# Two transformer layers with experts: the down projection from half-precision parts, and the queries of the second attention in another order

## The chip, the cores and the metric

## The reference, cut to what matters

x is 64 x 64 x 128 (4096 tokens of width 128), ctx the same. Four blocks, each added to x times a gate:

```python
x = x + tanh(g_xattn[0]) * pooled_attention(layernorm(x), ctx)
x = x + tanh(g_ffn[0]) * experts_relu(layernorm(x))      # top 2 of 8
x = x + tanh(g_xattn[1]) * cross_attention(layernorm(x), ctx, mask)  # 16 heads of 8
x = x + tanh(g_ffn[1]) * experts_gelu(layernorm(x))
```

An expert is `act(x @ W1 + b1) @ W2 + b2` with W1 128 x 512 and W2 512 x 128. In the first experts block each token goes to its two best of eight experts with their biases; in the second one the 8192 sorted pairs of token and expert are cut into eight equal parts, one for each expert's weights, without biases.

## The kernel before, in words

Tokens lie 128 to a slot in 32 slots (X), eight chunks of 512 tokens (c) or four pairs of chunks (p). The first attention and the first routing run until about 200 us. Routing scatters a row for each token and choice (its value as two f16 parts, its number and its weight) to a list in memory sorted by expert (xs).

**Experts.** `experts(l)` exists once for every engine (PE line 912, ACT 1183, DVE 1607, POOL 521, SP 640). It takes tiles of 256 rows: 40 in layer 0, 32 in layer 1, in rounds of eight; the first and the last round are written out, those between are a hardware loop, in which the semaphore values that are waited for depend on the loop's register. SP loads a tile's rows; PE transposes them (`gather`, line 929); DVE copies them to SBUF (`parts`, line 1614); PE multiplies with w1 in 12 f16 matmuls of 256 columns (`up`: w1 high times both halves of x, w1 low times the high half, four chunks of FF); ACT applies relu or gelu (lines 1195, 1198) and writes `hid` in f32; PE multiplies with w2 (`down`, lines 942 to 951) in eight f32 matmuls of 128 columns, which the trace records as two each; DVE adds the bias (layer 0, line 1297), multiplies with the weight (line 1632) and POOL scatters the result to ys (line 528), after a 1x1 operation (line 526) that tells DVE of its turn. All matmuls have line 758, the helper `mm`. Which expert a tile has is read from a table in SBUF into a register: on PE twice per tile (`expert`, line 954), in layer 0 on ACT (1193) and DVE (1626) as well. Weights are then addressed by `ds(e * FF + c * D, D)`. The order on PE is written out by hand (`round_`, line 956):

```python
gather(i, q + 1)
up(i, q, expert(i * XS_LEAD + q))
down(i, q - 1, expert(i * XS_LEAD + q - 1))
```

and on DVE (line 1635): `parts(i, q + 1)`, then `result(i, q - 1)`.

**Between the experts.** After layer 0 DVE fills half of `kmask` with zeros (line 1668), turns the mask and fills v9 (1671 to 1679); ACT fills both halves of `qmask` (1211); SP loads ys (660); POOL adds the two rows of a token (551); DVE adds them to x (`combine`), normalises pair by pair (`norm`: lines 1302 to 1323); PE transposes (`query_transposed`, 991) and projects (`query_projected`), ACT and DVE take the high and the low f16 part (1226, 1603), SP stores them and loads them back in the layout of the scores, for `q3` and, blanked by head, for `qmask`.

**The attention loop** runs over g from -8 to 41 on PE, ACT and DVE, one slot of 128 tokens per step. `scores(g + 6)` feeds a maximum over keys (line 1712) six steps ahead; every four maxima are turned, stored and loaded back (max_rows) as an additional row of the next product; `scores_by_key(g)` gives the exponential (1236). In the order of before all four pairs of queries are projected ahead of or in the first step (`query(p)`, line 1004), and the first `scores_by_key` waits for all low parts. Routing of layer 1 and the splitting of its w1 run inside this loop; its scatters end in a wait of all engines, from about 600 to 640 us, which ends when rewritten rows have been stored and loaded. In that wait the first tiles of layer 1 already run from rows gathered by POOL (`head_gathered`).

## Time and profile before

| | |
|---|---|
| runs | 770.82, 771.95, 767.83 us; median 770.82 |
| profiled execution | 765.61 us, its span 763.8 us, mean granted clock 0.795 |
| busy, share of the span | PE 68%, PEld 56%, DVE 55%, ACT 31%, POOL 44% |
| experts of layer 0, 205 to 348 us | PE busy 138.66 of 143 us, clock 0.98 |
| queries, 358 to 427 us | PE busy 37.8 of 69 us, DVE 46.7 |
| experts of layer 1 after the wait, 641.3 to 735 us | PE busy 93.16 of 93.7 us, clock 0.98 |
| chain that ended last | PE 50%, DVE 24%, POOL 8%, issue 8%, DMA 6% |

### The profile page before, as it was taken

How to read it: one execution, taken by the hardware profiler on the slowest of the kernel's cores; microseconds unless marked ns; L12 is line 12 of the kernel's file. 1: busy time of each engine (PE TensorE's matmuls, PEld its weight loads, DVE VectorE, ACT ScalarE, POOL GpSimd, SP SyncE). 2: the span in 40 equal slices, each digit the busy share in tenths (PEclk: the TensorE clock that was granted, in tenths of full speed). 3: DMA queues.
4: the chain of work that ended last, by engine and by line, in shares of the span. 5: the costliest groups of instructions: out<-in, count | busy, mean ns of one | idle time of the engine just before them, and what ended most of it. 6: DMA issues, size and time to landing. Idle time of an engine off the chain costs nothing.

```text
span 763.8 us, 17097 instructions
## 1 busy us (share of the span) xinstructions
PE 518.3 (68%) x5273; PEld 428.3 (56%) x5274; DVE 416.7 (55%) x1454; ACT 235.4 (31%) x411; POOL 339.5 (44%) x424
## 2 busy tenths in 40 slices
PE   1587958423199999992387687777862076999950
PEld 1255745301199899991254466666651065989950
DVE  4785686987123333334895377878568611222215
ACT  0221011222044444443621365454631021232310
POOL 6212106777345656665500000071647676666650
PEclk9978876755599999997565599696765578999995
DMA  7911101124222222342763265353214123232219
GB/s 210 264 32 42 28 1 44 51 95 129 69 72 79 76 79 73 80 136 76 236 187 124 55 162 151 96 150 71 67 45 147 45 54 101 80 79 80 68 52 317
DMA packets 73194, 76.51 MB, mean 100 GB/s; under 512 B 12984, under 2 KB 61368, under 8 KB 73064
## 3 DMA queue, kind: packets, MB, share of 16 engines
q1 hardware_dynamic: 58504, 50.98, 24.4%
q0 software_dynamic: 10224, 22.40, 9.5%
q10 hardware_dynamic: 4400, 2.26, 1.0%
q8 instruction: 40, 0.66, 0.4%
q14 instruction: 26, 0.21, 0.1%
HBM read 46.15 MB, written 29.34 MB: 99 GB/s over the span
## 4 chain that ended last, share of the span: by engine, by line
PE 50%; DVE 24%; POOL 8%; issue 8%; DMA 6%; ACT 2%; SPq 1%; POOLq 0%; ACTq 0%; DVEq 0%
PE PS L758 46%; POOL xs L517 5%; DVE XN L1323 3%; DVE stats L1302 3%; DMA work<-ys 3%; DVE X L1297 2%; PE PS L929 2%; DVE work L1712 2%; DVE work L1297 1%; POOL work L565 1%; DVE rtmp L1297 1%; DVE mv L1305 1%; DVE nwt L1297 1%; PE PS L1074 1%; DMA work<-max_rows 1%
## 5 line engine op out<-in xcount | busy, mean ns | idle before, releaser
L517 POOL DMA_INDIRECT xs<-pack,adr_i x80 | 78.7, 983 | 197.8 <-ACT pack L1147 142.0
L528 POOL DMA_INDIRECT ys<-work x144 | 140.7, 977 | 34.5 <-issue 34.5
L758 PE MATMUL PS<-w,work 128*128 x1152 | 143.8, 279 | 3.0 <-issue 1.7
L758 PEld LDWEIGHTS PS<-w,work 128*128 128x128 f32 x1152 | 134.9, 193 | 9.0 <-issue 6.8
L758 PE MATMUL PS<-work,w1h 128*128 128x256 f16 x576 | 103.1, 281 | 1.1 <-issue 1.1
L1195 ACT ACTIVATE work<-PS,b 128x256 f32<-128x256 f32 x160 | 62.7, 474 | 95.5 <-PE PS L758 69.2
L1297 DVE TENSOR_TENSOR work<-PS,work 128x256 f32<-128x256 f32 (+3 forms) x82 | 33.0, 405 | 94.7 <-issue 55.6
L758 PE MATMUL PS<-work 97*64 97x256 f16 (+5 forms) x608 | 74.0, 318 | 15.4 <-DVE work L1429 7.6
L758 PE MATMUL PS<-work,w1l 128*128 128x256 f16 x288 | 80.9, 281 | 0.0
L758 PEld LDWEIGHTS PS<-work 97*64 97x64 f16 (+2 forms) x608 | 56.0, 163 | 25.9 <-DVE work L1429 10.9
L1632 DVE TENSOR_SCALAR work<-PS,work 128x128 f32<-128x128 f32 x64 | 19.5, 346 | 79.0 <-PE PS L758 79.0
L929 PE MATMUL PS<-ident,work 128*128 128x128 f16 x288 | 29.5, 228 | 47.2 <-DMA work<-xs,headadr_i 24.6
L758 PEld LDWEIGHTS PS<-work,w1h 128*128 x576 | 54.7, 101 | 8.4 <-issue 2.1
L1712 DVE TENSOR_REDUCE work<-PS 128x16 f32<-128x1024 f32 x32 | 39.1, 1222 | 33.8 <-PE PS L758 33.8
L1198 ACT ACTIVATE work<-PS 128x1024 f32<-128x1024 f32 x32 | 32.8, 1024 | 80.2 <-PE PS L758 80.1
L758 PE MATMUL PS<-work,W 128*128 128x512 f32 x60 | 48.4, 933 | 8.1 <-DVE work L1297 3.4
L517 POOL DMA_INDIRECT xs<-work,adr_i x48 | 47.1, 981 | 14.8 <-issue 13.6
L1614 DVE COPY work<-PS 128x512 f16<-128x512 f16 x72 | 30.1, 418 | 39.7 <-PE PS L929 39.5
L929 PEld LDWEIGHTS PS<-ident,work 128*128 128x128 f16 x288 | 22.8, 102 | 50.7 <-issue 39.6
L526 POOL TENSOR_TENSOR turn<-lane 1x1 f32<-1x1 f32 x72 | 17.3, 240 | 72.6 <-DVE work L1632 72.4
L1236 ACT ACTIVATE XN<-PS,mask_bias 128x1024 f32<-128x1024 f32 x32 | 35.6, 1113 | 19.1 <-PE PS L758 18.9
L758 PE MATMUL PS<-ident,work 128*64 128x36 f32 x512 | 25.9, 255 | 22.7 <-DVE work L1297 22.7
(259 smaller groups left out, 809.8 us busy)
## 6 DMA issues: line engine op xcount, KB each, us to landing
work<-xs SPq DMA_DIRECT2D x132, 65.0 KB
work<-ys SPq DMA_DIRECT2D x12, 512.0 KB, 5.9
k_parts<-work SPq DMA_DIRECT2D x24, 128.0 KB
w<-k_parts SPq DMA_DIRECT2D x8, 384.0 KB
work<-k_parts SPq DMA_DIRECT2D x32, 96.0 KB
work<-q_parts SPq DMA_DIRECT2D x8, 384.0 KB
work<-q_parts SPq DMA_DIRECT2D x32, 96.0 KB
ys<-work POOLq DMA_INDIRECT x144, 2.3
```

The source lines that it names most:

```text
L517: g.indirect_dma_start(xs[l], bass.IndirectOffsetOnAxis(adr_i[:, k, T:T + 1], 0), pack_of(l, c)[:, s, k, :].bitcast(U32), None)\
L528: g.indirect_dma_start(ys[l], bass.IndirectOffsetOnAxis(xin[:, q, u, :].bitcast(U32)[:, D:D + 1], 0), yrow[:, q, u, :], None).then_inc(ff[ ...
L758: return t.matmul(o, lhsT, rhs, start=start, stop=stop, skip_group_check=True)
L929: ins = t.transpose(o[:, h, u, :], xin[:, q, u, h * D:(h + 1) * D], ident16[:])
L1195: ins = a.activation(hid[:, v, c, :], PF[:, b * 512 + c * TILE:b * 512 + (c + 1) * TILE], ACT.Relu, bias=b1[:, ds(e * FC + c, 1)], scale=1 ...
L1198: ins = a.activation(hid[:, v, :, :].rearrange("p c n -> p (c n)"), banks(b, 1024), ACT.Gelu, scale=1 / WSCALE)
L1236: a.activation(pexp[:, T % 2, :], banks(2, 1024), ACT.Exp, bias=mask_bias[:, T:T + 1]).then_inc(p_done, 1)
L1297: return v_.tensor_tensor(o, x, y, op)
L1302: ins = v_.bn_stats(stats[:, T, :], X[:, T, 0:D])
L1323: ins = v_.tensor_scalar(XN[:, slot + s, :], X[:, T, 0:D], mv[:, T, 0:1], rstd[:, T:T + 1], ALU.subtract, ALU.mult)
L1614: v_.tensor_copy(xgT[:, v, :, :].rearrange("p h n -> p (h n)"), PS[:, v, 0:TILE].bitcast(F16))\
L1712: v_.tensor_reduce(rmaxq[:, c % 2, s, :], banks(0, 1024).rearrange("p (h k) -> p h k", h=H), AX, ALU.max).then_inc(s_max, 1)
```

## The change

**Down from parts.** `hid` is written in f32 as before; ACT copies it to f16 (`hid_hi`), DVE forms `hid_lo` = hid - hid_hi in two halves of 128 rows (`low`), each with a semaphore step. w2 is scaled by 256 and split in place of XN into high and low f16 parts before each layer's experts, by ACT (`w2_hi`) and DVE (`split_w2`); gates and b2 carry the scale. `down` makes, for each half u, eight matmuls with `hid_hi` (high and low part of w2 for each of four chunks), waits for `lo`, and makes four with `hid_lo`. DVE's order per tile becomes `result(q - 2)`, `parts(q + 1)`, `low(q - 1)`.

**Blanking.** b2 is loaded after the first attention to another place; the mask's preparation, both halves of `kmask`, and w2's split come before layer 0's experts on DVE. One half of `qmask` is filled by DVE, with v9, once all rows of layer 0 are scattered; the other by ACT.

**Queries.** Pair 0 is projected first; pair 1 is transposed in the attention loop's first step and projected in its step g = -3, pair 2 at g = -1 and 0, pair 3 at g = 1. DVE's maxima 0 to 5 stand between combine, statistics, roots and rows of the pairs. The queries use only the first 16 slots of XN, in turn; banks differ, small tiles of the maxima move to `big1`. SP stores, loads keys, queries, blocks and w1 in the new order.

The diff, cut to its core:

```diff
-b2b = at(104, [E * D])
+b2b = at(44, [E * D])
...
+hid_hi = at(48, [2, FC, TILE], F16)
+hid_lo = at(68, [2, FC, TILE], F16)
+w2_parts = XN[:].rearrange("p t d -> p (t d)").bitcast(F16)
...
-BANK_Q, BANK_K, BANK_X3, BANK_LG = (2, 5), (4, 5), (3, 4), 6
+BANK_K, BANK_LG = (4, 5), 6
+BANK_X3, BANK_Q = (3, 4, 3, 4, 3, 4, 5, 7), (2, 5, 2, 5, 5, 7, 5, 7)
...
+    sp.wait_ge(x1_done, NC)
+    sp.dma_start(b2b, A["b2"].partition_broadcast(P)).then_inc(w_late, 16)
...
+    sp.wait_ge(mask_rows, 1)
+    sp.dma_start(mask_dram, mask16[:]).then_inc(mask_out, 16)
...
-    for c in range(2):
-        load_keys(c)
-    for c in range(NC):
+    def queries_stored(c):
...
-        if c == 1:
-            for k in range(2):
-                load_queries(k)
-            load_blocks(0)
-        elif c == 3:
-            load_blocks(1)
-    for c in range(NC):
...
+    sp.wait_ge(mask_out, 16)
+    load_keys(0)
+    y_load(0, 6)
+    y_load(0, 7)
+    load_keys(1)
+    queries_stored(0)
+    queries_stored(1)
...
+    load_queries(0)
+    load_queries(1)
+    load_blocks(0)
+    queries_stored(2)
+    load_keys(2)
+    load_queries(2)
+    queries_stored(3)
+    load_blocks(1)
+    queries_stored(4)
+    queries_stored(5)
+    w1_load(0)
+    for c in range(1, NC):
...
-        if c >= 1:
-            load_max(c)
+        load_max(c)
+        if c == 1:
+            w1_load(1)
...
-        w1_load(c)
+        if c == 1:
+            queries_stored(6)
+            queries_stored(7)
+        else:
+            w1_load(c)
...
-        if l == 1:
-            pe.wait_ge(w2_in, 16)
...
-            v, m = q % 2, (i + i0) * (XS_LEAD // 2) + q // 2
-            pe.wait_ge(f["hid"][v], m + 1)
+            v, m, tile = q % 2, (i + i0) * (XS_LEAD // 2) + q // 2, (i + i0) * XS_LEAD + q
+            if q == 0 and isinstance(i, int) and i == 0:
+                pe.wait_ge(w2_lo, (l + 1) * E)
+            pe.wait_ge(f["hi"][0], tile + 1)
...
+                o = PS[:, 6 + v, u * D:(u + 1) * D]
...
-                    ins = mm(PS[:, 6 + v, u * D:(u + 1) * D], hid[:, v, c, u * P:(u + 1) * P],
-                             w2[:, ds(e * FF + c * D, D)], start=c == 0, stop=c == FC - 1)
+                    for part in range(2):
+                        mm(o, hid_hi[:, v, c, u * P:(u + 1) * P],
+                           w2_parts[:, ds(e * 2 * FF + part * FF + c * D, D)], start=c + part == 0, stop=False)
+                pe.wait_ge(f["lo"][0], 2 * tile + u + 1)
+                for c in range(FC):
+                    ins = mm(o, hid_lo[:, v, c, u * P:(u + 1) * P],
+                             w2_parts[:, ds(e * 2 * FF + c * D, D)], start=False, stop=c == FC - 1)
...
+        if c >= 6:
+            pe.wait_ge(qk_lo, NC + c - 1)
+        if c == 7:
+            pe.wait_ge(nT_sb, 2)
...
-            ins = t.transpose(PS[:, BANK_X3[c % 2], s * P:(s + 1) * P], XN[:, c * CT_TILES + s, :], ident[:])
+            ins = t.transpose(PS[:, BANK_X3[c], s * P:(s + 1) * P], XN[:, slots(1, c).start + s, :], ident[:])
...
-        if c >= 2:
-            pe.wait_ge(qk_lo, NC + c - 1)
+        if 2 <= c < 5:
+            pe.wait_ge(qk_lo, NC + (0, 0, 1, 2, 4)[c])
+        if c == 5:
+            pe.wait_ge(v9_sb, 1)
...
-        mm(PS[:, BANK_Q[c % 2], :], wq1T, xnT1[:, c % 2, :]).then_inc(qk_ps, 1)
+        mm(PS[:, BANK_Q[c], :], wq1T, xnT1[:, c % 2, :]).then_inc(qk_ps, 1)
...
-    def query(p):
+    def queries_transposed(p):
...
+    def queries_projected(p):
...
-    for p in range(NP - 1):
-        query(p)
+    queries_transposed(0)
+    queries_projected(0)
...
-                pe.wait_ge(qk_lo, 2 * NC)
-                pe.wait_ge(zero, 1)
-                mm(WEIGHTED_PS, zrow[:, 0:P], zrow[:, 0:HG * SEQ])
+                pe.wait_ge(x3t_sb, 5)
+                pe.wait_ge(qk_lo, NC + 3)
...
+        if g == 0:
+            queries_projected(2)
...
-            query(NP - 1)
+            queries_transposed(1)
+        if g == -1:
+            queries_transposed(2)
+        if g == 1:
+            pe.wait_ge(zero, 1)
+            mm(WEIGHTED_PS, zrow[:, 0:P], zrow[:, 0:HG * SEQ])
+        if g == 2:
+            pe.wait_ge(qk_lo, 2 * NC)
...
+            if k == 1:
+                pe.wait_ge(qk_lo, NC + 6)
...
+        if g == 3 - LEAD:
+            queries_projected(1)
+        if g == 1:
+            queries_transposed(3)
+            queries_projected(3)
...
+        act.wait_ge(w_late, 16 * NL)
+        act.wait_ge(pack_lo, (l + 1) * NC)
+        if l == 1:
+            act.wait_ge(w2_in, 16)
+        for e in range(E):
+            a.activation(w2_parts[:, e * 2 * FF:e * 2 * FF + FF], w2[:, e * FF:(e + 1) * FF], ACT.Copy,
+                         scale=WSCALE).then_inc(w2_hi, 1)
...
-        act.wait_ge(w_late, 16 * NL)
...
-            v, m = q % 2, (i + i0) * (XS_LEAD // 2) + q // 2
+            v, m, tile = q % 2, (i + i0) * (XS_LEAD // 2) + q // 2, (i + i0) * XS_LEAD + q
...
-            wait(act, f["y"][v], m)
+            if not isinstance(i, int) or tile >= 2:
+                act.wait_ge(f["lo"][0], 2 * tile - 2)
...
+            act.wait_ge(f["hid"][v], m + 1)
+            wait(act, f["y"][v], m)
+            a.activation(hid_hi[:, v, :, :], hid[:, v, :, :], ACT.Copy).then_inc(f["hi"][0], 1)
...
-    for u in range(2):
-        blanked(qmask[:, u, :, :, :], q_blank)
-    for p in range(NP):
+    blanked(qmask[:, 0, :, :, :], q_blank)
...
+    def queries_transposed(p):
...
-            a.activation(xnT1[:, c % 2, :], PS[:, BANK_X3[c % 2], :], ACT.Copy).then_inc(x3t_sb, 1)
+            a.activation(xnT1[:, c % 2, :], PS[:, BANK_X3[c], :], ACT.Copy).then_inc(x3t_sb, 1)
...
+    def queries_high(p):
...
-            a.activation(q16[c][:, 0, :], PS[:, BANK_Q[c % 2], :], ACT.Copy, scale=QK_SCALE[0])\
+            a.activation(q16[c][:, 0, :], PS[:, BANK_Q[c], :], ACT.Copy, scale=QK_SCALE[0])\
...
+    queries_transposed(0)
+    queries_high(0)
+    queries_transposed(1)
...
+        if g == -1:
+            queries_transposed(2)
+        if g == 0:
+            queries_high(2)
...
+            if T == 0:
+                act.wait_ge(x_ff[0], 7)
...
+        if g == 3 - LEAD:
+            queries_high(1)
+        if g == 1:
+            queries_transposed(3)
+            queries_high(3)
...
+            v_.tensor_scalar(gt[:, 2:4], gt[:, 2:4], 1 / WSCALE, None, ALU.mult)
...
+        def low(i, q):
+            v, m = q % 2, (i + i0) * (XS_LEAD // 2) + q // 2
+            dve.wait_ge(f["hi"][0], (i + i0) * XS_LEAD + q + 1)
+            wait(dve, f["y"][v], m)
+            for u in range(2):
+                half = slice(u * P, (u + 1) * P)
+                tt(hid_lo[:, v, :, half], hid[:, v, :, half], hid_hi[:, v, :, half], ALU.subtract)                            .then_inc(f["lo"][0], 1)
...
+                if q >= 2:
+                    result(i, q - 2)
+                elif not first:
+                    result(i - 1, XS_LEAD + q - 2)
+                late = first and l == 1 and q == HEAD0 - 1
+                if late:
+                    low(i, q - 1)
...
-                    result(i, q - 1)
+                    if not late:
+                        low(i, q - 1)
...
-                    result(i - 1, XS_LEAD - 1)
+                    low(i - 1, XS_LEAD - 1)
...
+        result(rounds_ - 1, XS_LEAD - 2)
+        low(rounds_ - 1, XS_LEAD - 1)
...
+    def split_w2(l):
+        for e in range(E):
+            hi, lo = (w2_parts[:, (2 * e + part) * FF:(2 * e + part + 1) * FF] for part in range(2))
+            dve.wait_ge(w2_hi, l * E + e + 1)
+            v_.scalar_tensor_tensor(out=lo, in0=w2[:, e * FF:(e + 1) * FF], scalar=WSCALE, in1=hi,
+                                    op0=ALU.mult, op1=ALU.subtract).then_inc(w2_lo, 1)
...
-    v_.memset(kmask[:, 0, :, :, :], 0.0).then_inc(k_blank, 1)
-    experts(0)
-    dve.wait_ge(tails, 16 * E)
-    v_.memset(kmask[:, 1, :, :, :], 0.0).then_inc(k_blank, 1)
...
+    v_.tensor_scalar(b2b, b2b, WSCALE, None, ALU.mult)
+    split_w2(0)
+    v_.memset(kmask[:, 0, :, :, :], 0.0).then_inc(k_blank, 1)
+    dve.wait_ge(tails, 16 * E)
+    v_.memset(kmask[:, 1, :, :, :], 0.0).then_inc(k_blank, 1)
+    experts(0)
+    for q in range(XS_LEAD):
+        dve.wait_ge(ff["stored"][q], STORED * rounds[0])
...
-    for p in range(NP):
-        for c in (2 * p, 2 * p + 1):
-            combine(0, c)
+    v_.memset(qmask[:, 1, :, :, :], 0.0).then_inc(q_blank1, 1)
...
+    def maxima(T):
+        c, s = T // CT_TILES, T % CT_TILES
+        dve.wait_ge(s_ps, T + 1)
...
+        if s == CT_TILES - 1:
+            dve.wait_ge(s_max, T + 1)
...
+                dve.wait_ge(nT_ps, c)
+            link(v_.tensor_scalar(nmax.rearrange("p (r s j) -> p s r j", j=HG, r=HG),
...
+            tt(nmax16[:, 1, :], nmax, nmax16[:, 0, :], ALU.subtract).then_inc(n_ready, 1)
...
+    def query_rows(p):
+        if p >= 2:
+            dve.wait_ge(x3t_ps, 2 * p - 2)
+        norm_std(pair(p))
+        norm_rows(pair(p), slots(1, 2 * p).start, xn3)
...
+    for p in range(2):
+        combine(0, 2 * p)
+        combine(0, 2 * p + 1)
...
-        norm(pair(p), pair(p).start, xn3)
-        if p >= 1:
-            parts_of_projection(2 * p - 2)
-            parts_of_projection(2 * p - 1)
-    for g in range(G0, G1):
-        k = g + LEAD - 1
-        if k in (0, 1):
-            parts_of_projection(NC - 2 + k)
-        if k == 2:
+        norm_stats(pair(p))
+        if p == 1:
+            parts_of_projection(0)
+            parts_of_projection(1)
+        norm_root(pair(p))
+        if p == 1:
+            maxima(0)
+        query_rows(p)
+    maxima(1)
+    combine(0, 4)
+    maxima(2)
+    combine(0, 5)
+    maxima(3)
+    dve.wait_ge(x_ff[0], 6)
+    norm_stats(pair(2))
+    maxima(4)
+    parts_of_projection(2)
+    parts_of_projection(3)
+    norm_root(pair(2))
+    maxima(5)
+    query_rows(2)
+    combine(0, 6)
+    combine(0, 7)
+    dve.wait_ge(x_ff[0], 8)
+    norm_stats(pair(3))
+    parts_of_projection(4)
+    parts_of_projection(5)
+    norm_root(pair(3))
+    for g in range(G1):
+        if g == 2:
...
-            c, s = T // CT_TILES, T % CT_TILES
-            dve.wait_ge(s_ps, T + 1)
...
-            if s == CT_TILES - 1:
-                dve.wait_ge(s_max, T + 1)
-                if c >= 1:
-                    dve.wait_ge(nT_ps, c)
-                link(v_.tensor_scalar(nmax.rearrange("p (r s j) -> p s r j", j=HG, r=HG),
...
-                link(v_.tensor_copy(nmax16[:, 0, :], nmax))
-                tt(nmax16[:, 1, :], nmax, nmax16[:, 0, :], ALU.subtract).then_inc(n_ready, 1)
+            maxima(T)
+        if g == 0:
+            query_rows(3)
+        if g == 1:
+            parts_of_projection(6)
+            parts_of_projection(7)
```

## Rows read from the trace of the kernel before

**Rows 1.** The page's first part: busy us, share of the span, instructions.

```profile
PE 518.3 (68%) x5273; PEld 428.3 (56%) x5274; DVE 416.7 (55%) x1454; ACT 235.4 (31%) x411; POOL 339.5 (44%) x424
```

**Rows 2.** Windows: us, busy by engine, PE's granted clock, DMA share, GB/s.

```profile
265.10:292.70 27.60, 27.20 (x256) 25.45 (x256) 9.90 (x33) 12.53 (x32) 16.93 (x24) 1.00 0.28 77
641.30:735.00 93.70, 93.16 (x859) 87.20 (x860) 24.43 (x79) 27.64 (x27) 57.50 (x81) 0.98 0.27 74
...
378.00:403.00 25.00, 21.51 (x94) 14.93 (x94) 23.77 (x113) 7.28 (x13) 0.00 (x0) 0.70 0.56 172
403.00:427.00 24.00, 14.32 (x70) 9.30 (x69) 9.83 (x13) 3.22 (x6) 0.00 (x0) 0.50 0.45 134
```

**Rows 3.** Timeline of PE, layer 0: start, length, engine, line, operation, tiles, shapes, count.

```profile
226.50 0.27 PE L758 MATMUL PS<-work,w1l 128*128 128x256 f16 x1
226.61 1.95 PE L758 MATMUL PS<-w,work 128*128 x16
228.40 0.39 PE L929 MATMUL PS<-ident,work 128*128 128x128 f16 x4
...
229.93 1.95 PE L758 MATMUL PS<-w,work 128*128 x16
```

**Rows 4.** Source views, 640.2 to 643.6: count, duration ns, first and last start.

```profile
L758 PEldq FUSED_REGOPS  x4: 46/46/46, 641.2 to 641.9; - x4
...
L758 PEldq ALU_OP  x4: 32/32/32, 641.3 to 642.0; - x4
...
L954 PEldq TENSOR_LOAD <-eidx_i x2: 306/350/395, 640.3 to 642.3; - x2
...
L758 PEldq FUSED_REGOPS  x4: 46/46/46, 643.0 to 643.4; - x4
```

**Rows 5.** Source view of line 954 in a dense stretch of layer 1.

```profile
L954 PEldq TENSOR_LOAD <-eidx_i x3: 297/298/301, 688.6 to 691.9; - x3
```

**Rows 6.** Timelines of ACT, DVE and PE, layers 0 and 1.

```profile
227.49 1.56 ACT L1195 ACTIVATE work<-PS,b 128x256 f32<-128x256 f32 x4 [1.75 <-PE PS L758]
...
229.34 0.42 DVE L1297 TENSOR_TENSOR work<-PS,work 128x256 f32<-128x256 f32 x1 [2.05 <-PE PS L758]
...
230.20 0.42 DVE L1614 COPY work<-PS 128x512 f16<-128x512 f16 x1
...
686.27 1.95 PE L758 MATMUL PS<-w,work 128*128 x16
...
688.46 0.61 DVE L1632 TENSOR_SCALAR work<-PS,work 128x128 f32<-128x128 f32 x2 [2.38 <-PE PS L758]
```

**Rows 7.** Groups by line: busy us, mean ns of one, idle before.

```profile
L1297 DVE TENSOR_TENSOR pack<-XN,pack 128x512 f16<-128x512 f32 x10 | 6.8, 684 | 0.0
...
L1143 ACT ACTIVATE pack<-XN 128x512 f16<-128x512 f32 x10 | 6.1, 626 | 6.7 <-DVE XN L1323 6.7
```

**Rows 8.** Timeline of DVE at the start of layer 0.

```profile
205.24 0.42 DVE L1614 COPY work<-PS 128x512 f16<-128x512 f16 x1 [12.64 <-PE PS L929]
```

**Rows 9.** Timelines after layer 0, and the chain there (start, us, what).

```profile
350.21 4.29 POOL L526 TENSOR_TENSOR turn<-lane 1x1 f32<-1x1 f32 x1 [0.48 <-DVE work L1632]
...
350.92 3.47 DVE L1668 MEMSET work<- 128x4096 uint32 x1 [0.80 <-issue]
...
358.70 5.11 DMA work<-ys
```

**Rows 10.** Timeline of DVE at 373, and the chain from 400 to 440.

```profile
373.80 3.08 DVE L1323 TENSOR_SCALAR XN<-X,mv,rstd 128x128 f32<-128x128 f32 x8
...
415.41 1.24 DVE work L1712
...
421.19 5.73 DMA work<-max_rows
...
427.06 1.09 PE PS L758 x8
...
431.44 1.24 DVE work L1712
```

58 lines of the change are left out of this document (32 added, 26 removed).

## The prediction

> **What bounds the kernel now.** The page first: no engine is busy for more than 68% of the span [rows 1], so each stage has to be read by itself. The windows by stage [rows 2] show experts stages in which PE is busy 99% of the time at a granted clock of 1.00 and 0.98, which is the full one of its two levels (2.4 GHz); in the query stage between them DVE is busy 23.8 of 25 us and then 9.8 of 24, with PE at 0.70 and 0.50. So experts follow PE; the queries follow DVE, and after it a chain of waits.
>
> One tile in the timeline [rows 3]: up's last matmul, the 16 records of down, four transposes, the next down. Down starts at 226.61, the transposes at 228.40: 1.79 us for eight f32 matmuls, 0.112 a record. The next down starts at 229.93: **a tile is 3.32 us**. In the loop's rounds eight tiles (256 PE records) take 27.6 us, 3.45 each [rows 2].
>
> Behind the array stands its sequencer, whose rows (PEldq) are not counted as busy. After 640.3 the array had been idle, and nothing but its own work held the sequencer [rows 4]: it loads the expert's number at 640.3; up's eight address operations run from 641.2 to 642.0, 0.12 apart whether they take 46 or 32 ns; the second load is at 642.3; down's four run from 643.0 to 643.4, again 0.12 apart. With down's remainder (0.1) and the start of the next gather that is about 3.2 us a tile. In the dense stage its rhythm is that of the tile: three loads from 688.6 to 691.9, two per tile [rows 5]. **So array (3.32) and sequencer (3.2) are nearly equal**, and in loop rounds, where the thresholds of waits are register values too, the same matmuls already take 0.13 longer.
>
> **The change, part by part.**
>
> Down on the array: 24 f16 matmuls of 128 columns instead of 8 of f32. The nearest row has their shape, the four transposes: 0.39 for four of which the last one's 0.22 counts once, so 0.056 each [rows 3]. 24 x 0.056 = 1.34 against 1.79: the array would need 2.87 us a tile, 0.45 less. The Trainium skill ("TensorE: Matmul & The Clock Gate", Back-to-back issue gap) gives about 81 ns for a matmul of N=128 in a stream of load and matmul pairs; by that down would take 1.94, a tile of the array 3.5, and the sum below would be some 8 us higher, an estimate by that page. The row speaks against it, though for four in a row only.
>
> Down on the sequencer: weights are addressed by expert, part and chunk, eight addresses instead of four. Up shows one operation for two matmuls with the same address (8 for 12), down one for both u (4 for 8), so I count 4 more a tile: 4 x 0.12 = 0.5. A tile then needs 3.2 + 0.5 + 0.05 for two more waits = 3.75. Computed afresh at every use it would be 20 more, 2.4 us; hidden by something I don't see, 0. In loop rounds the thresholds tile + 1 and 2 tile + u + 1 are new in every tile, three more at 0.12: 3.35 + 0.5 + 0.36 = 4.2.
>
> Down's new inputs. ACT copies hid to f16 behind relu: 1024 elements, 1.05, from 0.63 for 512 [rows 7] with the fixed part taken once. In layer 0 relu starts at 227.49, 0.72 after up ends (226.50 + 0.27), since the expert's number is loaded there too, and takes 1.57: 3.4 in all, under the tile. In layer 1 1.02 and 1.05. DVE forms the low part in halves of 512 elements, 0.68 each [rows 7], 1.3 for both. Its order becomes result(q-2), copy(q+1), low(q-1); result waits for a down that waited for a low: **a ring DVE, PE, DVE**. In layer 0 [rows 6] down's end (226.61 + 1.95) to the add at 229.34 is 0.78, the add to the end of the copy is 1.28, low 1.3, less overlap: 3.3 from down's end to low's. In layer 1 down's end (686.27 + 1.95) to 688.46 is 0.24, then 0.9 and 1.3: 2.4.
>
> PE's side: from low's end the sequencer issues the last matmuls, gather, load, up's addresses, load, its 3.75 less the 1.0 of down's eight addresses = 2.75 until down can begin. Then eight matmuls paced by addresses (1.0), 16 at 0.056 (0.9), 0.2 to the end: 2.1. Between two turns of the ring lie two tiles: layer 0 (2.1 + 3.3 + 2.75)/2 = 4.1; layer 1 (2.1 + 2.4 + 2.75)/2 = 3.6, under the sequencer's 3.75. In loop rounds layer 0 has 0.4 of thresholds more per turn: 4.3.
>
> Experts in sum. Layer 0: 16 tiles x (4.1 - 3.32) + 24 x (4.3 - 3.45) = 12.5 + 20.4 = 33. Layer 1: six tiles run before 640 in the shadow of the rewritten rows; 10 x (3.75 - 3.32) + 16 x (4.2 - 3.45) = 4.3 + 12 = 16. In each layer's last tile copy, low and down stand in series, +1 each. **Together +51.** Bounds: with free addresses layer 0 still goes by DVE's part of the ring (3.3 + 0.4 = 3.7: +15) and layer 1 by the array (26 x 0.4 = -10), +5; with 20 operations +160.
>
> Moved ahead of layer 0 on DVE: mask work (1.3), b2's scaling (0.7), eight low parts of w2 (5.5, at 0.69), one more memset (3.5), 11 us in all. DVE has been idle for 12.6 us when the first tile's copy starts at 205.24 [rows 8], and PE and DVE wait there for the scatters: hidden, 1.6 to spare, and beyond that it delays the first tile. ACT's eight copies (0.63) run beside. Before layer 1 the same splitting lies in the wait that ends at 640.3: nothing. On SP b2's DMA moves behind the residual and ahead of the tails, the mask's store ahead of the wait for the scatters, y's chunks 6 and 7 between key loads, where they are used last: nothing, between 0 and +2.
>
> Memset after layer 0: a 1x1 operation on POOL took 4.29 [rows 9], over the whole of DVE's 3.47 memset, and the last scatter waited behind it. That memset is now earlier: -4.1. In return v9's memset (2.0) and one of qmask (3.5) run while y loads (5.1) and hold DVE and POOL's sums some: +1.8. ACT blanks for 7 us instead of 14, not waited for.
>
> Queries in the order of need. Before [rows 10], pair 0's rows end at 376.9, the other pairs follow, the maxima wait for them and the fourth ends at 416.65, and the first scores by key start at 427.06, 5.7 of the 10.4 us being DMA; the seventh maximum is at 431.4. After, by the same durations less 2.3: pair 0's rows to 374.6, low parts of chunks 0 and 1 to 380.4, pair 1's root to 383, first maximum at 387 after store and load, pair 1's rows and the maxima to 398.7, so the chain would allow 409. But DVE has 17 us for pairs 2 and 3 meanwhile, and comes to the seventh maximum at 417, -14.4; pair 3's rows and low parts (3.4) and PE's last pair (2) are then still to do. -9, the memset's in it; rounded to -10, between 0 and -22 (DVE's 14 idle us, the memset, part of the DMA chain).
>
> **Sum:** 765.6 (the profiled execution: span 763.8 and 1.8 around it) + 51 - 10 = 807. The runs' median of before is 770.8, 5 above that execution; I leave the 807.
>
> **Rivals.**
> *Addresses are hidden.* Then the experts cost +5 and the queries give up to 16: 755. For it: an operation is 46 ns long. Against: 0.12 apart even with an empty array. The place is PE's sequencer between low and up, and it decides if one address costs under 0.03.
> *It cancels:* half hidden (+25), queries at their bound (-22): 769.
> *The clock falls.* PE would work 2.87 of 4.1 us; 99% busy goes with 1.00, 21.5 of 25 with 0.70 [rows 2]. Matmuls at half clock add 1.6 a tile where it happens; in a third of 66 tiles +35: 842.
> *Every use computes its address:* about 920.
>
> **Chances.** Forecast 0.62 (785 to 828, its own range); as forecast but only to 775 to 785, 0.08; clock 0.08; every use 0.04; cancels 0.06; hidden 0.12. The range leaves out the last, the clock and every use but for their nearest parts: 768 to 828. 0.5% is about what a measurement can tell from no change. Faster 0.12, same 0.06, slower 0.82.
>
> **What would show it.** Twelve to sixteen address operations a tile at the matmul's line; tiles of 4.1 and 3.75 us, longer in loop rounds; PE busy under 85% there; eight matmuls of down spaced 0.12, the rest 0.056; the 4.29 on POOL gone; the seventh maximum 14 us nearer to layer 0's end. Tiles of 3.0 in layer 1 would say that the sequencer never was a bound and the forecast is wrong.

## The result, and the profile after

| | before | after |
|---|---|---|
| runs | 767.83 to 772.11, median 771.38 us | 833.45 to 837.97, median 833.75 us |
| ratio | | 1.083, 95% interval 1.078 to 1.088 |
| profiled execution, its span | 765.61, 763.8 | 833.45, 831.7 |
| mean granted clock | 0.795 | 0.803 |

The change costs 8.3%. The forecast was 807, and 833.75 lies above the range. The page's first part, to be held against [rows 1]:

```profile
PE 545.0 (66%) x5849; PEld 414.8 (50%) x5850; DVE 514.2 (62%) x1617; ACT 312.7 (38%) x498; POOL 366.8 (44%) x424
```

PE was given less array work a tile, and is busy longer. DVE gained 98 us, ACT 77. The groups name the new work and its pauses:

```profile
L780 PE MATMUL PS<-XN,work 128*128 (+1 forms) x2752 | 173.3, 230 | 27.9 <-issue 21.5
L533 POOL DMA_INDIRECT ys<-work x144 | 164.8, 1145 | 34.3 <-issue 34.3
...
L1375 DVE TENSOR_TENSOR work<-work 128x512 f16<-128x512 f32 (+1 forms) x152 | 98.9, 690 | 5.9 <-ACT work L1262 5.6
...
L1262 ACT ACTIVATE work<-work 128x1024 f16<-128x1024 f32 x72 | 76.1, 1057 | 2.3
```

Most of PE's pauses before down's matmuls end with "issue": no other engine was late, its own sequencer was. **One tile**, in the source view of a loop round of layer 0 (294.0 to 298.3; count, duration ns, first and last start). L780 is the helper that issues every matmul, so its thirteen operations are down's eight, four of up's and the first of the next down:

```profile
L780 PEldq FUSED_REGOPS  x13: 46/46/60, 294.0 to 298.2; - x13
...
L780 PEldq ALU_OP  x4: 32/32/32, 296.5 to 297.2; - x4
...
L982 PEldq TENSOR_LOAD <-eidx_i x2: 302/303/304, 295.6 to 297.4; - x2
```

So sixteen address operations a tile, eight for up and eight for down, and two loads. Windows of loop rounds of both layers (columns as in [rows 2]), of the stretch between first and fourth maximum, and of the queries that follow:

```profile
265.10:298.22 33.12, 28.91 (x305) 22.41 (x303) 18.31 (x47) 19.97 (x38) 18.73 (x23) 1.00 0.24 65
711.60:776.10 64.50, 56.77 (x605) 44.66 (x603) 32.11 (x76) 31.21 (x30) 37.35 (x46) 1.00 0.23 62
425.00:437.00 12.00, 5.30 (x32) 3.16 (x32) 8.49 (x18) 1.20 (x2) 0.00 (x0) 0.50 0.04 15
437.00:478.00 41.00, 31.69 (x181) 22.69 (x183) 22.70 (x85) 10.67 (x18) 0.00 (x0) 0.58 0.36 99
```

The clock stays at its full level in the experts with PE busy 87 and 88%. In the queries it is at the lower level, 1.2 GHz, or little above it in the mean.

**Where the 68 us between the two profiled spans lie**, by the starts of single instructions in both traces: first load of the first tile's expert number 206.80 to 213.31 (+6.5); from there to the last load of layer 0 136.7 to 170.1 (+33.4); to the first exponential 84.6 to 72.4 (-12.3); to the fifth 14.2 to 29.5 (+15.3); to the last 122.0 to 126.3 (+4.3); layer 1's tiles, from the load at 640.3 to the last one, 92.6 to 112.5 (+19.9); the rest +0.8.

Of the +6.5 some 5 are not the change's: from 62 to 86 us, where both kernels do the same, the granted clock was 0.72 in the execution of before and 0.61 in that of after, and it was 0.61 as well in a kernel of the experiments whose code up to there is that of before and whose first load comes at 212.0. The other 1.7 are the change's. While DVE splits w2, POOL's scatters of the routing take 1.4 to 1.5 us instead of 0.97:

```profile
196.31 1.51 POOL L522 DMA_INDIRECT xs<-work,adr_i  x1 [0.30 <-issue]
198.12 1.50 POOL L522 DMA_INDIRECT xs<-work,adr_i  x1 [0.30 <-issue]
```

From the first to the last of these 64 scatters 83.5 to 83.8 us pass in all six kernels that split w2 there, 81.9 to 82.4 in twelve of the thirteen that do not. **Experts +53.3, queries +7.** The forecast had +51 and -10. Of the queries' +7 the last +4.3, from the fifth exponential to the last, is no more than executions with the same instructions in that stretch differ by: 119.4, 122.0 and 126.2 us in the kernel before and two kernels that differ from it in the experts alone.

**The query stage** in the chain of waits (start, us, what), where [rows 10] stood before:

```profile
398.94 3.69 POOL work L556
...
424.80 1.22 DVE big L1802
...
437.49 7.81 PE PS L780 x28
445.39 1.22 DVE big L1802
...
454.73 4.08 PE PS L780 x20
...
462.55 1.22 DVE big L1802
...
469.84 11.65 PE PS L780 x92
...
497.74 4.13 issue
```

The first maximum now follows 35.4 us behind POOL's last turn in layer 0 instead of 53.0. Of these 17.6 us 4.1 are the last turn itself, which took 4.29 [rows 9] and now takes 0.15. Then the chain runs through PE: 7.8 us between the fourth and fifth maxima, 4.1 ahead of the seventh, 11.7 ahead of the fourth exponential, of which 7.0 are the projections of pair 3, in front of what the third waits for. PE's timeline says what stands there, the projections of pairs 1 and 3, each chunk 2.05 for the queries and 1.71 for the router's logits at half clock:

```profile
437.30 2.05 PE L780 MATMUL PS<-work,W 128*128 128x512 f32 x2
439.14 1.71 PE L780 MATMUL PS<-wrc,work 128*128 128x8 f32 x8
...
469.68 2.07 PE L780 MATMUL PS<-work,W 128*128 128x512 f32 x2
471.54 1.72 PE L780 MATMUL PS<-wrc,work 128*128 128x8 f32 x8
```

### The profile page after: what moved, and what is told of

Its sections match the earlier page's. It is cut to its first block, busy times and chain, and to the rows that moved or that the text cites. A ratio compares the mean times of both kernels' runs of the same rounds, so it can differ in the third digit from the quotient of the medians.

```text
span 831.7 us, 19026 instructions
## 1 busy us (share of the span) xinstructions
PE 545.0 (66%) x5849; PEld 414.8 (50%) x5850; DVE 514.2 (62%) x1617; ACT 312.7 (38%) x498; POOL 366.8 (44%) x424
## 4 chain that ended last, share of the span: by engine, by line
PE 51%; DVE 21%; issue 11%; POOL 8%; DMA 6%; ACT 2%; SPq 1%; POOLq 0%; ACTq 0%; DVEq 0%
PE PS L780 46%; POOL xs L522 5%; DMA work<-ys 2%; DVE big L1802 2%; DVE XN L1410 2%; DVE stats L1379 2%; PE PS L949 2%; DVE X L1375 2%; DVE work L1375 1%; POOL work L570 1%; DVE rtmp L1375 1%; PE PS L1023 1%; DVE mv L1385 1%; DVE nwt L1375 1%; PE PS L1110 1%
## 5 line engine op out<-in xcount | busy, mean ns | idle before, releaser
L780 PE MATMUL PS<-XN,work 128*128 (+1 forms) x2752 | 173.3, 230 | 27.9 <-issue 21.5
L533 POOL DMA_INDIRECT ys<-work x144 | 164.8, 1145 | 34.3 <-issue 34.3
L780 PEld LDWEIGHTS PS<-XN,work 128*128 128x128 f16 (+1 forms) x2752 | 136.7, 102 | 73.4 <-issue 55.4
L780 PE MATMUL PS<-work,w1h 128*128 128x256 f16 x576 | 102.2, 280 | 10.1 <-issue 8.1
L1375 DVE TENSOR_TENSOR work<-work 128x512 f16<-128x512 f32 (+1 forms) x152 | 98.9, 690 | 5.9 <-ACT work L1262 5.6
L780 PE MATMUL PS<-work 97*64 97x256 f16 (+5 forms) x608 | 78.1, 327 | 24.5 <-DVE work L1517 7.5
L780 PE MATMUL PS<-work,w1l 128*128 128x256 f16 x288 | 80.2, 278 | 0.0
L1262 ACT ACTIVATE work<-work 128x1024 f16<-128x1024 f32 x72 | 76.1, 1057 | 2.3
L780 PEld LDWEIGHTS PS<-work 97*64 97x64 f16 (+2 forms) x608 | 58.5, 168 | 35.9 <-DVE work L1517 10.8
L780 PEld LDWEIGHTS PS<-work,w1h 128*128 x576 | 51.7, 100 | 25.7 <-issue 19.1
L1802 DVE TENSOR_REDUCE big<-PS 128x16 f32<-128x1024 f32 x32 | 39.1, 1222 | 34.7 <-PE PS L780 34.6
L522 POOL DMA_INDIRECT xs<-work,adr_i x48 | 48.7, 1014 | 15.3 <-issue 13.7
L780 PE MATMUL PS<-work,W 128*128 128x512 f32 x60 | 48.9, 941 | 8.1 <-DVE work L1375 3.4
L949 PEld LDWEIGHTS PS<-ident,work 128*128 128x128 f16 x288 | 20.0, 102 | 49.5 <-issue 42.7
```

Of the source, the lines that this page charges most:

```text
L522: g.indirect_dma_start(xs[l], bass.IndirectOffsetOnAxis(adr_i[:, k, T:T + 1], 0), pack_of(l, c)[:, s, k, :].bitcast(U32), None)\
L533: g.indirect_dma_start(ys[l], bass.IndirectOffsetOnAxis(xin[:, q, u, :].bitcast(U32)[:, D:D + 1], 0), yrow[:, q, u, :], None).then_inc(ff[ ...
L780: return t.matmul(o, lhsT, rhs, start=start, stop=stop, skip_group_check=True)
L949: ins = t.transpose(o[:, h, u, :], xin[:, q, u, h * D:(h + 1) * D], ident16[:])
L1262: a.activation(hid_hi[:, v, :, :], hid[:, v, :, :], ACT.Copy).then_inc(f["hi"][0], 1)
L1375: return v_.tensor_tensor(o, x, y, op)
```

## The experiments

Theories for the experts: (1) PE's sequencer, by addresses, loads and thresholds, and in layer 0 a ring with DVE; (2) the array or the number of matmuls; (3) DVE's low parts alone. For the queries: PE's projections in the loop, the clock, DVE's memsets beside POOL, SP's order.

### The new query stage alone

Down, its inputs and `result` are put back to f32 in the changed kernel (`w2_parts`, `split_w2`, `low` and ACT's copies gone); the rest stays.

> The query stage of the changed kernel with the experts' down as before (f32, four addresses a tile, no parts of w2 or hid). What is left of the difference to before is the query stage alone. If the pieces read from the two traces are right (experts +53, query stage +7), the time is 833.75 - 53 = 780 us, about 8 above before. If the prediction's sum is right for the stage (-10) and the experts cost more than they show, it is 761. Tiles at 3.3 us again in both layers.

775.44 us against 767.59 of before, ratio 1.0104 (1.0058 to 1.0149). So the stage costs some 8 us and the experts 1.0831 - 1.0104, or 56. The reading of the traces holds, and the forecast's -10 is where it failed.

### Down's weights at a fixed address

```
-   w2_parts[:, ds(e * 2 * FF + part * FF + c * D, D)]
+   w2_parts[:, part * FF + c * D:part * FF + c * D + D]
```

> The changed kernel with down's weights always taken from expert 0 at addresses that are constants (that expert's weights stand in for the chosen one's; both loads of the expert's number stay). Eight address operations a tile are gone, 24 matmuls stay. Theory 1, PE's sequencer sets the tile: it falls from 4.15 by 8 x 0.12 = 1.0 to 3.2 in layer 1, and in layer 0 to the ring of DVE and PE at 3.6 to 3.7: 833.75 - 22 - 25 = 787 us. Theory 2, the array or the number of matmuls sets it: unchanged, 834. Theory 3, the ring with DVE's low parts sets both layers: layer 0 unchanged, at most -10.

Every tile is then multiplied with expert 0's w2, so the output is no longer that of the reference; number and shape of the instructions stay. 802.51 us, 1.0471 (1.0389 to 1.0552), 28 under the changed kernel by the ratios; expected were 47. The rate of the tiles is read from POOL's one small operation a tile, in the source view of its line, first over the 24 loop tiles of layer 0, then over the 16 of layer 1. Before the change:

```profile
L526 POOL TENSOR_TENSOR turn<-lane x24: 182/183/184, 244.5 to 323.6; 1x1 f32<-1x1 f32 x24
...
L526 POOL TENSOR_TENSOR turn<-lane x16: 182/183/183, 661.1 to 712.5; 1x1 f32<-1x1 f32 x16
```

After the change:

```profile
L531 POOL TENSOR_TENSOR turn<-lane x24: 182/183/184, 259.1 to 357.5; 1x1 f32<-1x1 f32 x24
...
L531 POOL TENSOR_TENSOR turn<-lane x16: 182/183/184, 711.6 to 776.1; 1x1 f32<-1x1 f32 x16
```

With the fixed address:

```profile
L531 POOL TENSOR_TENSOR turn<-lane x24: 182/183/184, 253.4 to 346.1; 1x1 f32<-1x1 f32 x24
...
L531 POOL TENSOR_TENSOR turn<-lane x16: 182/183/641, 697.6 to 748.6; 1x1 f32<-1x1 f32 x16
```

Span over count less one: 3.44 and 3.43 before, 4.28 and 4.30 after, 4.03 and 3.40 here. Layer 1 gives back 0.90 a tile for eight addresses, 0.11 each, with all 24 matmuls still there: theory 1, against 2. Layer 0 gives back 0.25 only: there something else stands at 4.0.

### Rounds written out; one load a tile

```
-   with pe.Fori(1, n - 1) as i:
+   for i in range(1, n - 1):
```

and the same on SP, ACT, DVE and POOL.

> The changed kernel with the rounds of tiles written out instead of looped, on every engine: the thresholds of waits are constants, the addresses stay. Theory 1 (sequencer, thresholds at 0.12 each, about 3 a tile on PE): 24 tiles of layer 0 give 0.1 to 0.3, 16 of layer 1 0.4: 833.75 - 6 to - 14, so 820 to 828 us. If thresholds are free: 834.

821.31 us, 1.0677 (1.0582 to 1.0773), 12 under the changed kernel. Loop tiles are 4.11 and 3.85, by the same rows as above.

```
-   down(i, q - 1, expert(i * XS_LEAD + q - 1))
+   down(i, q - 1, numbers[q - 1])
```

> The changed kernel with the expert's number kept in its register from up to the down of the same tile, so that PE loads it once a tile instead of twice (seven of eight tiles). Theory 1 (sequencer: a load holds it 0.6 to 0.75 us): tiles from 4.15 to 3.5; in layer 0 the ring with a PE part of 2.0 instead of 2.75 gives 3.7: 833.75 - 16 - 17 = 800 us. Theory 2 (array) or 3 (DVE): at most -5.

814.36 us, 1.0606 (1.0506 to 1.0706), 17 under. Loop tiles 4.13 and 3.77; layer 1's last eight come at 3.20, from 3.74. So loops and loads are the sequencer's as well: in layer 1 0.45 a tile for the thresholds and whatever else a loop costs, 0.53 for seven eighths of a load. Layer 0 stays at 4.1 in both, which fits the prediction's ring.

### The ring in layer 0

Both edits together, and in layer 0 DVE's `low(i, q - 1)` ahead of `result(i, q - 2)`.

> The changed kernel with rounds written out, one load of the expert's number a tile, and in layer 0 DVE's low part of a tile ahead of the result of the tile before it. Theory 1 (sequencer in layer 1, DVE's ring in layer 0): layer 1's tiles go to 3.2 to 3.3 us, layer 0's from 4.1 to the ring by ACT (up 1.7, two ACT operations 3.4, down 2.2, over two tiles: 3.65) or a little above, 3.75: 833.75 - 20 - 18 = 795 us, 1.035 of before. Theory 2, layer 0 is held by ACT or POOL already: layer 0 stays at 3.9 to 4.1, 805 us, 1.045. Layer 1 at the array's 2.87 would say that only the sequencer held it, 3.2 that something else is near.

793.48 us, 1.0349 (1.0304 to 1.0394), as expected:

```profile
L531 POOL TENSOR_TENSOR turn<-lane x24: 182/183/185, 251.6 to 337.6; 1x1 f32<-1x1 f32 x24
...
L531 POOL TENSOR_TENSOR turn<-lane x16: 183/185/732, 687.1 to 736.9; 1x1 f32<-1x1 f32 x16
```

3.74 and 3.32. The result of the tile before, its load of the expert's number included, had stood between ACT's copy and the low part for which PE waits. Layer 0's tile falls by 0.37 from the 4.11 of written-out rounds alone, but most of that is not the new order's. The first and the last round are written out in the kernel with one load as well, so they have both edits without the order: turns there are 3.86 and 3.87 apart (the layer's last tile left out), with the order 3.81 and 3.76. So the order is worth 0.05 to 0.1 a tile, and the rest is what the two edits give together. That the ring of DVE and PE sets layer 0 is argued from its sum, not shown by this run. Layer 1 does not reach the array's estimated 2.87, and the window of its last tiles in the kernel with one load (columns as in [rows 2]) has a candidate for what is next:

```profile
763.00:785.00 22.00, 20.30 (x252) 17.86 (x249) 14.33 (x33) 12.48 (x12) 17.53 (x21) 1.00 0.17 52
```

POOL is busy 17.5 of 22 us, and with the pauses that end with "issue" between its operations (0.5 a tile) it has under 0.2 a tile left: two scatters of 1.15 each, a turn of 0.25. Before the change a scatter took 0.98. Two other readings remain. The sequencer's own 3.74 less 0.57 for the load is 3.17; but with the fixed address, which takes 0.9 from the sequencer, the last tiles are no faster, at 3.22. And whether PE or ACT would go on at 3.2 with shorter scatters was not tried.

### Was the sequencer the bound before?

```
+   expert(i * XS_LEAD + q)
    up(i, q, expert(i * XS_LEAD + q))
```

in the kernel before.

> The kernel before with one load more of the expert's number on PE in each tile, its value not used. Nothing else changes. This tests the premise of the prediction, that PE's sequencer (3.2 us a tile) stands just behind the array (3.32) before the change. Theory 1: a load holds the sequencer 0.6 to 0.75 us, so it becomes the bound at 3.8 to 3.95: 40 tiles of layer 0 and 26 of layer 1 take 0.4 to 0.5 more, +26 to +33 us, 1.034 to 1.043 of before. Theory 2, the sequencer had slack, the array stays the bound: +0 to +5, 1.000 to 1.006.

808.7 us, 1.0554 (1.0489 to 1.062), +42: above both expectations. Tiles:

```profile
L526 POOL TENSOR_TENSOR turn<-lane x24: 182/183/185, 252.9 to 347.3; 1x1 f32<-1x1 f32 x24
...
L526 POOL TENSOR_TENSOR turn<-lane x16: 182/183/183, 689.1 to 751.0; 1x1 f32<-1x1 f32 x16
```

4.10 and 4.13, so +0.66 and +0.70 for one load; where two loads follow each other they start 0.65 apart. Nothing was hidden: in loop rounds the sequencer was not just behind the array but the bound itself. In the written-out last rounds the tile grows by 0.5 to 0.6 (3.32 to 3.81, 3.19 to 3.77), so there it did have about 0.1 of slack, as the prediction said. The counterpart takes from it, in the kernel before, by rounds written out and one load a tile:

> The kernel before with rounds of tiles written out and one load of the expert's number a tile (seven of eight). The prediction's reading was that PE's sequencer (3.2 us a tile) stands just behind the array (3.32) and loses 0.13 a tile in loop rounds. If so: 24 tiles x 0.12 in layer 0 and 16 x 0.1 to 0.2 in layer 1 come off, -4 to -6: 0.993 to 0.995 of before. If the array alone sets the tile, or DVE and ACT in loop rounds: 1.000.

```profile
L526 POOL TENSOR_TENSOR turn<-lane x24: 182/184/185, 248.8 to 325.2; 1x1 f32<-1x1 f32 x24
...
L526 POOL TENSOR_TENSOR turn<-lane x16: 182/183/184, 663.3 to 713.1; 1x1 f32<-1x1 f32 x16
```

3.32 in both, the array's tile, 0.12 under before in the mean of the 40 loop tiles. Before, most of that lies where one round ends and the next begins: turns there are 4.27 to 4.41 apart, the others mostly 3.2 to 3.6. So it is mostly one pause of about 1 us a round, not 0.13 at every tile's thresholds. The time, 762.76 us against 770.14 with a ratio of 0.9975 (0.9923 to 1.0026), shows no gain that is clear of noise.

### The memsets moved ahead of layer 0, alone

```
+   v_.memset(kmask[:, 0, ...], 0.0).then_inc(k_blank, 1)
+   dve.wait_ge(tails, 16 * E)
+   v_.memset(kmask[:, 1, ...], 0.0).then_inc(k_blank, 1)
    experts(0)
```

with the mask work, b2's load and the mask's store moved as in the change.

> The kernel before, with one part of the change alone: the mask work and both memsets of kmask ahead of layer 0 on DVE (b2's load moved behind the residual and the mask's store ahead of the tails, as the change has them). The prediction's step: the moved work is hidden in the wait for the scatters, and the 4.29 us that POOL's last turn took are gone: -4, 767 of 771 (0.995 of before). Rival: the y load, not the memset, ends last, or the moved work delays the first tile: 1.000 or above.

760.95 us against 768.05, 0.9903 (0.9865 to 0.994). A gain, under 2%, and by its interval somewhat more than the 4 us of the expectation. In the chain of waits POOL's last turn, 4.29 in [rows 9], is an ordinary one:

```profile
354.84 0.18 POOL turn L526
355.02 0.16 issue
355.18 0.98 POOL ys L528
```

and the first maximum follows 49.1 us behind it instead of 53.0.

### DVE's memset beside POOL's sum

In the kernel of the new stage alone ACT zeroes both halves of qmask.

> The same kernel (new query stage, f32 down), with ACT zeroing both halves of qmask as before the change, so that DVE has only v9's memset left while y loads. Theory 1: DVE's memsets hold POOL's first sum of y at 3.69 us instead of 1.25: -1 to -3.5 us, 1.006 to 1.009 of before. Theory 2: the y load ends last there: unchanged, 1.010. If ACT's second zeroing (5 to 7 us) reaches its first copy of the queries: slower.

773.63 us, 1.0093 (1.0061 to 1.0125): not to be told from 1.0104. The row it was about did change. POOL's second sum of y after the change, and DVE's memset over it:

```profile
398.94 3.68 POOL L556 TENSOR_TENSOR work<-work 128x512 f32<-128x512 f32 x1 [0.21 <-DMA work<-ys]
...
397.50 3.47 DVE L1797 MEMSET work<- 128x4096 uint32 x1 [0.92 <-issue]
```

and here:

```profile
359.13 1.64 POOL L556 TENSOR_TENSOR work<-work 128x512 f32<-128x512 f32 x1 [0.21 <-DMA work<-ys]
```

2.0 us less at that place, too little for the times.

### The clock

28 and then 6, 6, 6 matmuls of 256 columns ahead of the first four scores, in the kernel of the new stage alone.

> The kernel of the run with f32 down (new query stage alone, 1.0104 of before), with extra matmuls on PE where it waits: 28 of 256 columns ahead of the first scores, 6 ahead of each of the next three, into a PSUM bank that is overwritten later. Nothing is left out. Theory 1: the projections of pair 1 run at half clock because PE has idled before; with the clock up they take 3.5 instead of 7.0 us, and as they delay the fifth scores the stage gives back 3.5 (up to 8 if the clock stays up): 1.000 to 1.006 of before. Theory 2, DVE's order sets the stage: unchanged, 1.010. If the extra matmuls are themselves in the way: 1.015 or more.

778.1 us, 1.0146 (1.0102 to 1.019): no gain, and rather a loss. The windows show that PE's clock did rise for the projections of pair 1, and was down again for those of pairs 2 and 3:

```profile
390.00:400.00 10.00, 7.36 (x52) 4.26 (x51) 7.04 (x16) 0.78 (x2) 0.00 (x0) 0.84 0.01 3
400.00:410.00 10.00, 6.58 (x34) 4.88 (x32) 5.97 (x24) 1.96 (x4) 0.00 (x0) 0.67 0.28 66
410.00:420.00 10.00, 9.11 (x33) 5.98 (x33) 5.40 (x19) 3.42 (x5) 0.00 (x0) 0.50 0.74 226
```

Pair 1 took 4.9 us (397.64 to 402.56) instead of 7.0; pair 2, 3.9 us in the kernel after the change, took 7.0. What one place gained the next lost. What the stage would take at full clock throughout, no run shows.

### The logits out of the chain, and SP's order

```
    mm(PS[:, BANK_Q[c], :], wq1T, xnT1[:, c % 2, :]).then_inc(qk_ps, 1)
-   for s in range(CT_TILES): ... wrc ...
+   (for pairs 1 to 3: behind scores(g + LEAD) of g = -1, 0, 2)
```

> The kernel of the new query stage alone (f32 down, 1.0104 of before), with PE's small matmuls for the router's logits of pairs 1 to 3 (8 columns each, 1.7 us a chunk at half clock) taken from between the projections to behind the next scores, and DVE's use of them one turn later. Nothing is left out. Theory 1, PE's projections in the loop lie in series between maxima and exponentials: each of three places in the chain gives up to 3.4 us: -7 to -10, 0.998 to 1.002 of before. Theory 2, DVE's order or the loads of q and max_rows end last there: at most -2, 1.008 to 1.010.

771.92 us, 1.0103 (0.9991 to 1.0215), the time of the kernel without the edit. DVE's use of the logits moves with them, to one step later. From POOL's last turn to the third exponential 81.8 us pass, against 88.3 in the changed kernel (88.6 with the extra matmuls, 89.2 with ACT's zeroing); to the ninth 110.1 against 113.6; to the last 222.4 against 222.2. The gain of 6 to 7 us is gone by the end of the stage. The wait that took a part of it, in the chain:

```profile
427.68 9.84 PE PS L780 x92
...
453.71 4.97 issue
```

"Issue" here is a DMA that the chain doesn't name. In the kernel after the change the same place is a wait of PE's sequencer of 4.5 us at `scores_by_key`, for the rows of maxima, and SP's timeline says why they are late: the six stores of chunks 6 and 7 and four block loads go first.

```profile
487.11 2.97 SPq L601 DMA_DIRECT2D q_parts<-w1l  x6
490.19 3.46 SPq L682 DMA_DIRECT2D work<-q_parts  x4
493.75 1.21 SPq L448 DMA_DIRECT2D max_rows<-big  x2
497.68 0.29 SPq L451 DMA_DIRECT2D work<-max_rows  x1
```

```
    load_max(c)
+   if c == 2: queries_stored(6); queries_stored(7)
    ...
-   if c == 1: queries_stored(6); queries_stored(7)
```

> The kernel of the new query stage alone (f32 down, 1.0104 of before), with that move on SP alone. Theory 1, SP's order is a term of its own, beside PE's projections: -3, 1.006 of before. Theory 2, with the projections in series PE comes so late that the rows of maxima are no longer missed: 1.010.

774.14 us, 1.0079 (1.0057 to 1.01).

> The kernel of the new query stage alone with both: the logits behind the next scores and the stores of chunks 6 and 7 later. The logits alone brought exponential 2 nearer by 8 us, of which the wait for the rows of maxima took most back. Theory 1: both together give 8 + 3 = 11 us, 0.996 of before, and the stage is then some 3 us shorter than that of before, the prediction's gain in part. Theory 2, DVE or another load takes it back once more: 1.005 or above.

765.18 us, 0.9976 (0.9947 to 1.0005). Alone each edit is worth 0 to 2 us by the ratios (that of the logits has a wide interval), together about 10. The traces agree: the ninth exponential follows POOL's last turn by 113.6 us in the changed kernel, 110.1 with the logits later, 109.2 with SP's order, 100.5 with both, and the last one by 222.2, 222.4, 219.6 and 211.3. The projections and the rows of maxima end at the same place, and whichever is mended, the other is still late. SP's timeline now has the store of maxima when they are ready, 2.6 us ahead of the load, and the queries' stores behind:

```profile
443.81 1.24 SPq L448 DMA_DIRECT2D max_rows<-big  x2
446.37 0.28 SPq L451 DMA_DIRECT2D work<-max_rows  x1
446.69 4.30 SPq L601 DMA_DIRECT2D q_parts<-w1l  x6
```

Now those stores stand ahead of the next query blocks, and PE waits for these, in its timeline:

```profile
459.28 1.08 PE L780 MATMUL PS<-work 97*64 97x256 f16 x8 [2.11 <-DMA work<-q_parts]
```

From the eleventh to the twelfth exponential 9.0 us pass instead of 4.4 before and after the change, so SP's queue is still in the chain, and what is left of the head start goes there: from POOL's last turn the ninth exponential comes at 100.5, against 103.9 in the run with the old order of queries and the early memsets, the twelfth at 115.6 against 114.3, the last at 211.3 in both.

### Everything together

On the changed kernel (f16 down): rounds written out, one load, low first, ACT zeroes qmask, logits and stores later.

> The changed kernel, f16 down and all, with everything found: rounds written out, one load a tile, low part first in layer 0 (1.0349 of before so far), and the stage mended (ACT zeroes qmask, logits later, the stores of chunks 6 and 7 later). If the stage's terms are independent of the experts': 12 us less, 1.019 of before; layer 0's tiles 3.74 and layer 1's 3.2 to 3.3 as they were.

779.97 us, 1.0159 (1.014 to 1.0179). With f32 down instead (and DVE's order per tile as before the change), first without and then with SP's order:

> The same with ACT zeroing both halves of qmask, rounds of tiles written out and one load of the expert's number a tile, f32 down: the changed kernel's query stage mended, on the experts' part of before. By theory 1 (the logits later -8, the zeroing -1, loop thresholds at 0.12 each and sequencer -5): 8 - 14 = -6 us, 0.992 of before. By theory 2: 1.001.

764.22 us, 1.0026 (0.9964 to 1.0089).

> The kernel with f32 down, rounds written out, one load a tile, ACT zeroing both halves of qmask and the logits later (1.0026 of before), with one move more: SP stores the queries of chunks 6 and 7 behind the maxima rows of chunk 2 instead of ahead of its query blocks. Theory 1, SP's queue (3.0 us of stores, then 3.5 of block loads) makes the rows of maxima of chunk 2 late and PE waits 4.5 us for them: -3 to -4, 0.997 to 0.999 of before, and exponential 4 to 8 back from 16.7 to 14 us. Theory 2, another transfer is late next: unchanged.

759.2 us against 767.62, **0.9882 (0.9859 to 0.9904)**, under before by its interval, though by less than 2%, and by some 7 us more than expected. Where those come from stays open: beside the profiled execution of the kernel without the move, the ninth exponential is 2.4 us nearer to POOL's last turn and the last one not at all. The 779.97 of the kernel with f16 down is 21 us more, so down from parts loses even with all that was found. And the old order of queries with the early memsets, rounds written out and one load:

> The kernel before with the mask work and both memsets of kmask ahead of layer 0 (0.9903 alone), rounds written out and one load a tile. If both gains hold and add: 0.983 to 0.986 of before, 756 us. If the second is nothing: 0.990.

754.4 us against 770.14, 0.9898 (0.981 to 0.9986). The two can't be told apart, and neither can this one and the early memsets alone (0.9903). No run shows a gain of the order of need, mended, over the old order with the same memsets: equal here, and with looped rounds 0.9976 against 0.9903.

## Why the prediction was wrong, point by point

**Direction and mechanism of the experts were right.** "Array (3.32) and sequencer (3.2) are nearly equal": the sequencer was the bound in loop rounds already. Four more addresses and three more thresholds give tiles of 4.30 in layer 1's loop rounds (4.2 forecast) and 3.74 in its last ones (3.75); layer 0 4.28 in loop rounds (4.3) and 3.98 in its last eight (4.1). Layer 0 +33.4 (33), layer 1 +19.9 (16 and the last tile's 1): **+53.3 for +51**. That layer 0 came out by the ring's sum is as forecast; the ring itself is the part that no run isolates. The rival "addresses are hidden" is refuted by the fixed address, "every use computes its address" by the count of sixteen, and "the clock falls" by 1.00 in both windows. PE's busy share is 87 to 88%, the prediction had said under 85.

**The array's term.** 24 matmuls at 0.056 were taken from four transposes. In the dense part of down they stand 0.056 apart: 15 starts from 295.08 to 295.86 in the tile shown. The Trainium skill ("TensorE: Matmul & The Clock Gate", Back-to-back issue gap) has 81 ns for such pairs; the trace does not agree, and by that rule layer 1 with one load could not have reached 3.20.

**Moves ahead of layer 0: nearly hidden, and -4 from POOL's turn.** The run with the mask work and memsets alone shows no delay and a gain of 5 to 10 us; it is the one part of the change that pays. The splitting of w2, put at nothing as well, stretches POOL's scatters and costs 1.7 us.

**The step that failed** is "Queries in the order of need", which was to bring -10 and brought about +8. As the same kernel has the early memsets, worth -7 us by their own run (0.9903), the new order itself costs about 15 by the ratios (10 to 11 by the traces, to the last exponential). The step's first half was right: the first maximum comes 17.6 us nearer to the experts' end. Then the prediction let DVE's 17 us of work end the stage, "and comes to the seventh maximum at 417, -14.4", with "PE's last pair (2)" behind. The seventh maximum came 6.4 nearer (its end 80.3 us behind the last load of layer 0, 86.7 before), not 14.4. (The row at 431.44 in [rows 10] is the eighth, the prediction misnamed it; the eighth came 5.5 nearer.) PE's pairs were priced at 2, or not at all where they lay inside DVE's time. Pairs 1 and 3 take 7.0 each at the clock that [rows 2] had shown for the stage, 0.50 to 0.70, pair 2 3.9, and each lies between a maximum that PE has to wait for and scores or roots that wait for it: pieces of 7.8, 4.1 and 11.7 us of the chain. Moved behind the next scores, half of that work leaves the chain (6 to 7 us to the third exponential). And SP's queue got six stores ahead of a transfer with a due time. The prediction's "nothing, between 0 and +2" was for other moves on that queue; these stores it did not price at all. They take back the other gain until they are moved too. The two together are what the runs put in place of the failed term: 1.0104 to 0.9976, about 10 us. That leaves about 8 of the 18 us between forecast and result. By the traces the stage, mended, only equals the old one with the same memsets; SP's queue is late again at the twelfth exponential, but no run mends that, so what those 8 us are stays open. The extra matmuls, with the clock up for pair 1 alone, gave no gain; a clock at its full level throughout stays untested.

**The memsets while y loads** were put at +1.8. The 3.69 us in the chain is 2.0 more than the sum takes without them: right.

**The sum** was made against an execution of 765.6 while before's median is 771.4: that alone is 6 us of the 27 that are missing, the experts' term 2, the query stage's 18. That the 765.6 was a low one is chance: it is an execution with the higher of the two early clocks named above, which is worth 5 us by the start of the first tile.

## What to carry to other kernels

Count a sequencer's work as an engine's: each distinct dynamic address, each index load, each wait threshold from a register. Where its rhythm equals the tile's, less array work buys nothing and one more address costs its full price; adding one load to the old kernel would have shown it in one run. Ask also what a vector operation beside the general engine's scatters does to them. When work is moved into a loop of engines that wait for each other, price it at the clock of the place it moves to, ask for each piece which waits it lies between, and do the same for every transfer put ahead of one with a due time: two such delays that end together hide each other, and mending one shows nothing.
